# Four graph layers on one core: the first layer's states by 32x32 blocks and DMA instead of TensorE, and its low parts on GpSimd

## The reference

```python
# L0: normalized graph convolution
y = einsum('nm,bmf->bnf', adj, x) + x
y = einsum('bnf,fo->bno', y, weight) + bias
y = y / maximum(sqrt(sum(y * y, axis=2, keepdims=True)), 1e-12)
# L1: five gated steps (in_matrix = out_matrix = adj)
m = einsum('nm,bmd->bnd', adj, h); av = concat([m, m]); u3 = h @ u3_w.T + u3_b
z = sigmoid(av @ w3_w.T + w3_b + u3); r = sigmoid(av @ w4_w.T + w4_b + u3)
hv = tanh(av @ w5_w.T + w5_b + (r * h) @ u5_w.T + u5_b)
h = (1 - z) * h + z * hv
# L2: degree-normalized adjacency, then a linear map
out = einsum('nm,bmc->bnc', d[:, None] * (adj + I) * d[None, :], x) @ W.T + b
# L3: softmax over chosen values; the diagonal share on x @ W[0], the rest on x @ W[1]
```

## Time and profile before

| | |
|---|---|
| three runs | 721.05, 721.40, 721.72 us; median 721.4 |
| profiled execution | 721.18 us, of which the span on the core 719.4 |
| busy | PE 710.3, PEld 596.7, DVE 626.9, ACT 510.5, POOL 263.3 us |
| DMA moved | 57.60 MB, mean 80 GB/s |

### The profile page before, as it was taken

One profiled execution on the slowest core, in us unless ns is written; L12 is line 12 of the kernel. 1 busy time (PEld: TensorE's weight loads), 2 busy tenths in 40 slices (PEclk: granted clock), 3 DMA queues, 4 the chain that ended last, 5 costly groups with the idle time before them and its releaser, 6 DMA issues.

```text
span 719.4 us, 11592 instructions
## 1 busy us (share of the span) xinstructions
PE 710.3 (99%) x3468; PEld 596.7 (83%) x3472; DVE 626.9 (87%) x1463; ACT 510.5 (71%) x1057; POOL 263.3 (37%) x384
## 2 busy tenths in 40 slices
PE   9999999999999999999999999999999999999996
PEld 7888888888887888888888888888888888888886
DVE  5899798999997889898888888888899999999985
ACT  4799878876676876677666766667587857875443
POOL 1878411322211232222222111222122258779774
PEclk9999999999999999999999999999999999999999
DMA  6600004334446345335344444430000000176742
GB/s 211 247 1 2 1 16 88 84 82 93 96 103 166 83 81 105 86 79 146 85 88 89 89 88 89 88 74 1 1 1 1 1 1 2 16 162 151 200 119 88
DMA packets 185758, 57.60 MB, mean 80 GB/s; under 512 B 168416, under 2 KB 169952, under 8 KB 185184
## 3 DMA queue, kind: packets, MB, share of 16 engines
q1 hardware_dynamic: 185168, 56.86, 33.1%
q10 hardware_dynamic: 528, 0.00, 0.0%
HBM read 29.30 MB, written 25.44 MB: 76 GB/s over the span
## 4 chain that ended last, share of the span: by engine, by line
PE 88%; ACT 5%; DMA 3%; DVE 2%; issue 1%; POOL 0%; SPq 0%; POOLq 0%; ACTq 0%; DVEq 0%
PE agg_ps L1193 15%; PE agg_ps L1195 14%; PE agg_ps L1194 14%; PE gate_ps L1105 7%; PE gate_ps L1109 7%; PE gate_ps L1106 7%; PE cand_ps L1105 5%; PE cand_ps L1109 5%; PE cand_ps L1106 5%; PE gate_ps L1114 3%; PE cand_ps L1114 3%; DMA state_blocks<-cand 2%; ACT feat L598 1%; PE turn_ps L1235 1%; ACT res L505 1%
## 5 line engine op out<-in xcount | busy, mean ns | idle before, releaser
L693 POOL TENSOR_TENSOR nat_lo<-nat_lo,nat_hi 128x512 fp32r<-128x512 f32 x61 | 80.0, 1312 | 288.9 <-ACT agg_hi L534 288.9
L1193 PE MATMUL agg_ps<-adj_hi,nat_hi 128*128 128x512 f32 x384 | 153.5, 400 | 0.0
L1195 PE MATMUL agg_ps<-adj_hi,nat_lo 128*128 128x512 f32 x384 | 149.8, 390 | 0.0
L1194 PE MATMUL agg_ps<-adj_lo,nat_hi 128*128 128x512 f32 x384 | 149.6, 390 | 0.0
L909 DVE TENSOR_TENSOR agg_lo<-agg_ps,agg_hi 128x512 fp32r<-128x512 f32 x80 | 55.0, 688 | 44.8 <-ACT agg_hi L534 44.8
L559 ACT ACTIVATE gate_r<-gate_ps,bias 128x512 f32<-128x512 f32 x80 | 55.2, 690 | 50.0 <-PE gate_ps L1109 50.0
L534 ACT ACTIVATE agg_hi<-agg_ps 128x512 fp32r<-128x512 f32 x80 | 48.2, 603 | 54.7 <-PE agg_ps L1195 54.6
L1195 PEld LDWEIGHTS agg_ps<-adj_hi,nat_lo 128*128 128x128 f32 x384 | 72.1, 188 | 15.3
L1194 PEld LDWEIGHTS agg_ps<-adj_lo,nat_hi 128*128 128x128 f32 x384 | 72.2, 188 | 13.9
L1193 PEld LDWEIGHTS agg_ps<-adj_hi,nat_hi 128*128 128x128 f32 x384 | 72.3, 188 | 13.7
L735 POOL TENSOR_TENSOR rstd<-mean_var,half 128x4 f32<-128x4 f32 x62 | 69.9, 1127 | 5.2
(11 more groups left out here) (208 smaller groups left out, 1761.1 us busy)
## 6 DMA issues: line engine op xcount, KB each, us to landing
state_blocks<-cand SPq DMA_DIRECT2D x77, 256.0 KB, 2.1
nat_lo<-state_blocks SPq DMA_DIRECT2D x244, 64.0 KB, 2.5
res<-in_x SPq DMA_DIRECT2D x16, 256.0 KB, 5.8
feat<-state_blocks SPq DMA_DIRECT2D x64, 64.0 KB, 2.6
out<-res SPq DMA_DIRECT2D x16, 256.0 KB, 2.4
rows<-in_adj SPq DMA_DIRECT2D x4, 256.0 KB, 5.0
adj_hi<-eye_hi SPq DMA_DIRECT2D x1, 1024.0 KB, 9.3
adj_lo<-eye_lo SPq DMA_DIRECT2D x1, 1024.0 KB, 11.2
```

The source lines that it names most:

```text
L693: pool.tensor_tensor(flat(nat_lo[:, u % B, :, :]), flat(nat_lo[:, u % B, :, :]).bitcast(F32), flat(nat_hi[:, u % B, :, :]).bitcast(F32), A ...
L1193: pe.matmul(ps, nat_hi[:, b, k, :], m_hi[:, k, :], start=(k == 0), stop=False)
L1194: pe.matmul(ps, nat_hi[:, b, k, :], m_lo[:, k, :], start=False, stop=False)
L1195: last = pe.matmul(ps, nat_lo[:, b, k, :], m_hi[:, k, :], start=False, stop=(k == T - 1))
```

## The change

1. **L0's rows to states.** The turns "back" are gone from PE and ACT. DVE transposes 32x32 blocks of `res` into `early_staged` (units 0 to 8) or `late_staged` in the slot in which PE transposed before, SP stores them and, a slot later, loads them into `feat` with four DMAs.
2. **Low parts of L0 on POOL.** `nat_lo` of the inputs 3 to 15 is made by POOL in slot n-2 (semaphore `x_low_made`), and `nat_lo` of L0's results for the steps also by POOL, one slot after ACT's high part (`back_low_made`). DVE no longer makes either.
3. **Other inner states too.** Units 16, 78 and 79 go by blocks and DMA as all others.
4. **Quarters.** Both 1 MB loads into `later` are four DMAs of 256 KB, one a slot; `SUM_AT` is one slot later.

```diff
-BY_DMA = range(17, 78)
-SWAPPED = [*BY_DMA, *range(AFTER, AFTER + B)]
+SWAPPED = [*range(B, LAST), *range(AFTER, AFTER + B)]
-SUM_AT = VALUE_AT[-1] + 3
+SUM_AT = VALUE_AT[-1] + 4
...
-    found += [("back", u) for u in norms_at(s, "cross") if stage(u) == L0]
...
+            def back(n):
+                sp.wait_ge(back_swapped, n + 1)
+                sp.dma_start(swap_dram[n], staged(n)).then_inc(back_out[n % 2], 16)
+
+            def back_to_rows(n):
+                sp.wait_ge(back_out[n % 2], 16 * (n // 2 + 1))
+                if n >= 2:
+                    sp.wait_ge(back_in[n % 2], 16 * BLOCKS * (n // 2))
+                rows_of = swap_dram[n].rearrange("(q d) (k a i) -> a d k q i", q=BLOCKS, k=T, a=BLOCKS)
+                for j in range(BLOCKS):
...
+                    sp.dma_start(to, rows_of[j]).then_inc(back_in[n % 2], 16)
...
+                k = s - LATE_AT[-1] - 1
+                if 0 <= k < T:
+                    sp.wait_ge(late_added, T)
+                    if k:
+                        sp.wait_ge(rows_again, 16 * k)
+                    sp.dma_start(later[:, k, :], adj.rearrange("(p t) m -> t p m", t=T)[k]).then_inc(rows_again, 16)
...
# ACT
-                for n in norms_at(s, "back"):
-                    if stage(n) == L0:
-                        k = TURN_NO["back", n]
-                        act.wait_ge(turned, k + 1)
-                        act.activation(feat[:, n, :], turn_ps[k % 2][:, :], ACT.Copy).then_inc(turn_read_act, 1)
...
# POOL
+                if s + 2 < B and s:
+                    pool.wait_ge(x_hi_made, s + 3)
+                    pool.tensor_tensor(flat(nat_lo[:, s + 2, :, :]), flat(res[:, s + 2, :, :]),
+                                       flat(nat_hi[:, s + 2, :, :]).bitcast(F32), ALU.subtract).then_inc(x_low_made, 1)
+                for n in norms_at(s - 1, "split"):
+                    if stage(n) == L0:
+                        pool.wait_ge(split_hi_made, nth(SPLIT, n))
+                        pool.tensor_tensor(flat(nat_lo[:, n, :, :]), flat(res[:, n, :, :]),
+                                           flat(nat_hi[:, n, :, :]).bitcast(F32), ALU.subtract).then_inc(back_low_made, 1)
...
# DVE
+                    if stage(n) == L0:
+                        wait_normed(dve, n)
+                        if n >= 2:
+                            dve.wait_ge(back_out[n % 2], 16 * (n // 2))
+                        if n == STAGED_HIGH + 1:
+                            dve.wait_ge(agg_done, B)
+                        dve.transpose(staged(n), flat(res[:, n, :, :])).then_inc(back_swapped, 1)
-                if s + 3 < B:
-                    x_lo(s + 3)
...
# PE
-                    if s < B:
+                    if s < 3:
                         pe.wait_ge(x_lo_made, s + 1)
+                    elif s < B:
+                        pe.wait_ge(x_low_made, s - 2)
+                    elif s < 2 * B:
+                        pe.wait_ge(back_low_made, s - B + 1)
```

More of the change, by code:

```diff
@@ L170, with swap_lag @@
 Z_BEHIND = 0
-TURNED = [u for u in range(B, LAST) if u not in BY_DMA]
 def swaps(u):
     return sum(v <= u and v % 2 == u % 2 for v in SWAPPED)
-def read_by_act(turn):
-    return turn[0] == "back"
+def swap_lag(u):
+    return 3 if is_step(u) else DOWN_AT
 def reads(k):
-    return sum(read_by_act(x) == read_by_act(TURNS[k]) for x in TURNS[:k + 1])
+    return k + 1
+STAGED_HIGH = 8
 def nth(order, u):
@@ L342, in graph_layers, with staged @@
         l2_hi_made, mix_hi_made = sem("l2_hi_made"), sem("mix_hi_made")
+        def staged(n):
+            return (early_staged if n <= STAGED_HIGH else late_staged)[:, n % 2, :]
         def sums(n):
@@ L578, in slot @@
                     act.activation(reset_hi[:, :], gate_r[:, u % 2, :], ACT.Copy).then_inc(reset_hi_made, 1)
[L579 to L585, removed]
                 u = s - SWAP_LAG
-                if u in BY_DMA:
+                if is_inner(u):
                     act.wait_ge(swap_in[u % 2], 16 * BLOCKS * swaps(u))
@@ L911, in slot @@
                 u = s - 3
-                if u in BY_DMA:
+                if is_step(u) and u in SWAPPED:
                     dve.wait_ge(state_made, u - B + 1)
@@ L944, in slot @@
                                       ALU.add).then_inc(state_made, 1)
-                u = s - STATE_LAG
-                if is_inner(u) and u not in BY_DMA:
-                    dve.wait_ge(state_hi_made, nth(TURNED, u))
-                    dve.tensor_tensor(nat_lo[:, u % B, :, :],
-                                      turn_ps[TURN_NO["state", u] % 2][:, :].rearrange("p (t d) -> p t d", t=T),
-                                      nat_hi[:, u % B, :, :].bitcast(F32), ALU.subtract).then_inc(turn_read, 1)
                 for n in norms_at(s, "stats"):
@@ L1227, in slot @@
                     if k >= 2:
-                        if read_by_act(TURNS[k - 2]):
-                            pe.wait_ge(turn_read_act, reads(k - 2))
-                        if k - 1 > sum(map(read_by_act, TURNS[:k - 1])):
-                            pe.wait_ge(turn_read, sum(not read_by_act(x) for x in TURNS[:k - 1]))
-                    if kind in ("state", "result"):
+                        pe.wait_ge(turn_read, reads(k - 2))
+                    if kind == "result":
                         pe.wait_ge(state_made, i - B + 1)
@@ L1235, in slot @@
                             last = pe.transpose(to[:, t * P:(t + 1) * P], feat[:, i % B, t * P:(t + 1) * P], ident[:, :])
-                    elif kind == "back":
-                        wait_normed(pe, i)
-                        for t in range(T):
-                            last = pe.transpose(to[:, t * P:(t + 1) * P], res[:, i % B, t, :], ident[:, :])
                     elif kind == "adj":
```

73 lines of the change are left out of this document (40 added, 33 removed).

## The result

The changed kernel takes 734.55 us (median of six, 733.84 to 737.84) against 721.93 for the kernel before, run beside it. The ratio is 1.0183, 95% interval 1.0168 to 1.0199: slower by 12.6 us. The forecast was 731.8 (724.0 to 738.5). The profiled execution took 733.84 us, its span is 732.1.

A forecast was written before the change was run, and what follows sets the result against it. The prediction took PE, busy 99%, as the bound before, and POOL as the limit in L0 after the change. On 721.18 us it added +15.5 (slot 19), -3.8 (turns after it) and -1.1 (quarters): 731.8, range 724 to 738.5.

The forecast's parts named there:

- POOL has no room at PE's new pace: In L0, POOL's own slot takes 3.63 us against PE's 3.62 without a turn, before any work is added.
- POOL's slots of 5.03 and 6.43: L0: POOL's 3.63 us plus one subtraction of 1.40, or two from slot 8 on; input 15 ready at 80.5.
- second way: Unit 15's length from above: 86.5 less 12.3 idle plus 21 subtractions of 1.40 gives 103.6; taken as 102.
- Free at about 24.0, lengths and slot 19: POOL free at about 24.0 after unit 0's length; unit 15's length ends at 102, slot 19 starts at 104.0, 15.5 late.
- -3.8 after slot 19: After slot 19 POOL's slot is shorter than PE's, PE sets the pace, and eight turns of 0.48 us fall away.
- The quarters, -1.1: Loading 1 MB in quarters removes PE's stop of 1.11 us at 231.12; 0 as the other bound.
- POOL hides its new work: Rival: POOL's added subtractions in L0 cost no time and PE's pace holds, 711.0 us; chance 8%.
- The subtraction costs 1.89: Rival: each of 21 POOL subtractions costs as at 645.74, +10, 742 us; chance 5%.
- The lateness is half made up: Rival: POOL's lateness is half of that forecast, 723 to 724 us; chance 7%.
- PE's clock falls: Rival: PE's stops in slots 9 to 14 lower its clock to 1.2 GHz, about +8, 739 us; chance 7%.
- The rule on GpSimd's price: The skill's 2.6 cycles an element gives 1.11 us per POOL subtraction and 725.7 us; the trace's 1.31 was used.

The follow-up runs named there:

- all_low_on_dve: Changed kernel with the low parts of both inputs and L0's results made by DVE again; 720.50 us, ratio to the kernel before 0.9978-0.9998.
- clear_of_port_2: Changed kernel; from slot 19 results' subtractions wait for their own slot's `agg_hi`, swapped states' of slots 23 and 25 go ahead of the previous slot's statistics; 732.81 us.
- late_before_stats: Changed kernel; only the first nine results' low parts on POOL, three slots before use, in slots 19, 21, 23, 25 ahead of the previous slot's statistics; 717.00 us.
- clear_of_port: Changed kernel, but in slots 19, 21, 23 and 25 POOL's subtraction waits for the next slot's `agg_hi`; 736.46 us.

## Why the prediction was right, step by step

- **POOL has no room at PE's new pace.** Right, and shown by undoing it (all_low_on_dve). ACT and DVE, costed at nothing, cost nothing here because POOL's lateness covers them, as the prediction said; with POOL free, DVE is the limit. Input 8 was forecast for 38.3 and was ready at 38.32; PE was forecast to wait there and did.
- **POOL's slots of 5.03 and 6.43.** They were 4.70 and 5.94. The subtraction was sized nearly right (1.25 to 1.38 by starts, forecast 1.40); what was too long is POOL's own part, 3.63 from the earlier trace rows, which is 3.33 here (38.41 to 41.74). The prediction put the long small operations (0.64 against 0.23) down to a wait before them, or to their being "cold", and used them only to doubt its second way. The rows of the kernel before do not bear this out: behind the longest wait the operation takes 0.23, and where it takes 0.76 it starts together with DVE's own subtraction, which has two inputs in SBUF:

```profile
47.79 0.76 POOL L716 TENSOR_SCALAR length<-length 128x4 f32<-128x4 f32 x1 [0.65 <-ACT feat L598]
52.79 0.23 POOL L716 TENSOR_SCALAR length<-length 128x4 f32<-128x4 f32 x1 [1.08 <-ACT feat L598]
```

```profile
47.80 0.66 DVE L977 TENSOR_TENSOR nat_lo<-res,nat_hi 128x512 fp32r<-128x512 f32 x1
```

In the changed kernel DVE has no such subtraction there, and all 16 `length` operations of L745 take 0.22 to 0.24. In the slot of 3.63 itself the effect is small (`shift` beside DVE's subtraction takes 0.33 at 33.11, 0.24 in the changed kernel); the rest of the 0.30 was not traced. Input 15 was ready at 77.4, not 80.5.
- **Free at about 24.0, lengths and slot 19.** POOL's first two subtractions took 4.64 and 1.27 us (from 13.87 on; the first beside DVE's scan of 4.43 us, which ended at 17.44), so POOL was free at 25.16. With the shorter slots unit 15's length ended at 99.05, not 102, and by then POOL was no longer saturated: it stood idle 2.33 us for ACT's `feat` (L619) before that length. The 2.0 us from there to slot 19 held: 101.06, 12.6 us late for a forecast of 15.5. This is the term that was too large, by 2.9.
- **-3.8 after slot 19.** Failed: "POOL's slot is shorter than PE's, and PE sets the pace again" took POOL's spare time as proof that its work costs nobody anything. Slots 51 to 84 gave the 0.8 of two states back; slots 19 to 28, worth -2.9 by the forecast, gave +0.8, since POOL's subtractions lengthen DVE's operations. clear_of_port_2 shows the mechanism in slots 20 to 24 (-2.0). With no subtraction of L0 on POOL (all_low_on_dve) slots 19 to 28 take 57.08 us, 1.3 under the kernel before, and with them well placed (late_before_stats) 55.90, 2.4 under it: most of the 2.9 was to be had. The Trainium skill ("GPSIMD Engine Reference", section "8. Key points") names contention between GpSimd and VectorE instructions with two SBUF inputs; these runs agree and price it at up to 0.4 us for the subtraction and 1.1 for DVE's operation. The kernel before already has such pairs (the plainest: POOL at 134.61, 1.74 us; DVE's `feat_lo` at 135.11, 1.79), so the prediction could have read it there.
- **The quarters, -1.1.** -1.40 at slot 41; the stall behind `row_d`, which grew from 0.5 to 2.3 us, was missed, and took it back.
- **The sum.** Forecast +15.5 - 3.8 - 1.1 = 10.6; measured 12.56 + 0.10 = 12.66. The term at slot 19 was 2.9 too large and what follows it 5.0 too small: two errors cancelled in part, and the closeness of 731.8 to 734.6 is to that extent luck.
- **The rivals.** "POOL hides its new work" falls. "The subtraction costs 1.89" falls: it takes 1.7 to 1.8 only where it starts beside such an operation of DVE. "The lateness is half made up" falls. "PE's clock falls" came true in part: over slot 11 (53.7 to 59.6) the granted clock is 0.71 and over slot 15 (77.5 to 82.7) 0.67, behind slots in which PE stood 2 us of 5.9, and it is 1.00 between them:

```profile
47.80:53.70 5.90, 3.90 (x20) 3.19 (x20) 4.17 (x20) 4.54 (x19) 5.40 (x9) 1.00 0.29 68
53.70:59.60 5.90, 5.51 (x20) 4.36 (x20) 5.52 (x17) 3.91 (x15) 5.41 (x9) 0.71 0.52 109
59.60:65.60 6.00, 3.92 (x21) 3.23 (x21) 4.50 (x17) 4.00 (x15) 5.50 (x9) 1.00 0.54 109
```

(stretch, length, PE, PEld, DVE, ACT and POOL busy, granted clock, DMA share, GB/s). In slot 11, part of which went at the level of 1.2 GHz, it cost nothing: PE was busy longer, its wait for POOL fell from 2.01 to 0.43 us, and the slot stayed at 5.94. Slot 15 took 5.24 us (3.66 in clear_of_port, at the same place of the same program), and slot 19 still came no later than there. The rival's price assumed slots that run at 1.2 GHz from end to end and outlast POOL's; in L0 no slot did. Where POOL does not set the pace a slow stretch may cost time, as slot 18 of late_before_stats suggests.
- **The rule on GpSimd's price.** By the estimate of 1.11 us from the Trainium skill ("GPSIMD Engine Reference", section "Elementwise — side-by-side cycle accounting") the sum was 725.7. The new rows show 1.27 to 1.30, 1.25 to 1.38 by starts, and 1.74 under contention: the trace's price holds.

## What to carry to other kernels

Before work moves to an engine with a low share over the whole span, compare its own slot with the new pace in the stretch where the work lands; here 37% over the span was 75% there. The fastest run moved fewer subtractions (nine of 29) and issued each a few slots later. Spare time on GpSimd is not free time either: put its operations beside VectorE's operations that read PSUM or have one input. When a wait moves by a slot, list which operations then follow each other on the queue; two runs here missed their aim for that alone.

## What the hardware showed unexpectedly

- A 128x512 fp32 subtraction on GpSimd takes 1.30 us beside a PSUM operation or a transposition of VectorE, and 1.74 where it starts just behind the start of one with two inputs in SBUF. Such an operation of VectorE that starts while the subtraction runs ends 0.55 us after it (127 of 127 places in the two kernels), so it takes up to 1.78 instead of 0.68.
- Operations of 128x4 on GpSimd take 0.20 to 0.24 us, the power 1.04, and up to 0.76 and 1.63 beside such an operation of VectorE (kernel before, 47.79 and 72.77): the six of a slot make 3.3 us, more than two subtractions.
- A DMA of 512 elements of 4 bytes takes 9.9 to 11.8 us to land and delayed a 256 KB store issued beside it: ScalarE's wait for that store was 1.2 to 3.4 us.
